# Rotary value projection by Strassen's scheme in a fused perceiver kernel

## The reference, cut to what matters

```python
lat, ctx = layer_norm(latents), layer_norm(context)      # context: 2 x 2048 x 512
q = lat @ Wq                                             # 16 heads of 64
k, v = split(ctx @ Wkv, 2)                               # Wkv: 512 x 2048, so v = ctx @ Wv, Wv 512 x 1024
k = apply_rope(k, cos, sin)
attn = softmax(clip(q @ k.T * 64 ** -0.5, -11, 11))
x = x + (attn @ v) @ Wo + bo
```

## Time and profile before

| | us |
|---|---|
| median of 3 runs (1192.87 to 1197.12) | 1193.29 |
| the profiled execution, its own time | 1196.15 |
| its span, first to last instruction | 1194.4 |

### The profile page before, as it was taken

The page is one execution under the profiler, slowest core; times in us unless marked ns, Lnnn a source line. Parts: engine busy times, 40 slices in busy tenths (PEclk is TensorE's granted clock), DMA queues, the critical chain, the costliest instruction groups (busy, mean ns, idle before and its releaser), DMA issues.

```text
span 1194.4 us, 23415 instructions
## 1 busy us (share of the span) xinstructions
PE 1174.4 (98%) x9888; PEld 963.8 (81%) x9888; DVE 688.8 (58%) x1220; ACT 540.1 (45%) x907; POOL 217.0 (18%) x178
## 2 busy tenths in 40 slices
PE   8999999999999999999899999999999999999998
PEld 6888888888788888864546667888899999999997
DVE  4654554545464533466788885265765566566562
ACT  4433324332433322224359997373644544444441
POOL 2243343444333443350000000010000000000000
PEclk9999999999999999999989999999999999999999
DMA  8210201010100020245232324301545445445440
GB/s 302 71 55 1 66 2 52 4 36 19 36 19 2 27 72 1 83 139 212 96 152 79 136 108 178 142 1 72 228 159 211 161 192 211 157 195 207 158 162 19
DMA packets 28160, 126.06 MB, mean 106 GB/s; under 512 B 2715, under 2 KB 2971, under 8 KB 17572
## 3 DMA queue, kind: packets, MB, share of 16 engines
q1 hardware_dynamic: 28068, 124.74, 27.9%
HBM read 124.20 MB, written 0.52 MB: 104 GB/s over the span
## 4 chain that ended last, share of the span: by engine, by line
PE 49%; issue 2%; DVE 2%; ACT 2%; DVEq 0%
PE mid_bk L57 11%; PE mid_bk L58 10%; PE mid_bk L59 10%; PE mid_bk L1105 5%; PE mid_bk L1120 2%; PE mid_bk L1150 2%; PE mid_bk L1076 2%; PE mid_bk L995 2%; PE mid_bk L1140 1%; PE mid_bk L1249 0%; ACT sa_sc L1415 0%; PE mid_bk L1201 0%; PE mid_bk L1190 0%; PE mid_bk L1050 0%; PE mid_bk L986 0%
## 5 line engine op out<-in xcount | busy, mean ns | idle before, releaser
L565 POOL TENSOR_TENSOR norm_both<-norm_both,prob 128x512 f32<-128x512 f32 x118 | 155.4, 1317 | 145.6 <-DVE prob L357 138.2
L494 ACT ACTIVATE prob<-u_ps 128x512 f32<-128x512 f32 x128 | 66.2, 605 | 181.5 <-PE u_ps L667 181.5
L57 PE MATMUL mid_bk<-mo_x_hi,mo_w_hi 128*128 128x256 f32 x496 | 141.0, 284 | 0.0
L58 PE MATMUL mid_bk<-mo_x_lo,mo_w_hi 128*128 128x256 f32 x496 | 141.0, 284 | 0.0
L59 PE MATMUL mid_bk<-mo_x_hi,mo_w_lo 128*128 128x256 f32 x496 | 141.0, 284 | 0.0
L340 DVE TENSOR_TENSOR turned<-k_ps,tabs 128x512 f32<-128x512 f32 x32 | 22.1, 690 | 189.7 <-PE k_ps L59 189.6
L1788 DVE TENSOR_TENSOR mo_w_lo<-w_raw,mo_w_hi 128x2048 fp32r<-128x2048 f32 x32 | 73.3, 2292 | 72.7 <-ACT mo_w_hi L1497 72.7
L57 PE MATMUL k_ps<-ctx_hi,wk_hi 128*128 128x512 f32 x256 | 102.8, 402 | 0.0
L57 PE MATMUL u_ps<-wv_hi,ctx_hi 128*128 128x512 f32 x256 | 101.7, 397 | 0.8 <-ACT prob L494 0.8
L483 ACT ACTIVATE vals<-u_ps 128x512 f32<-128x512 f32 x64 | 38.3, 598 | 141.2 <-PE u_ps L59 141.1
L1497 ACT ACTIVATE mo_w_hi<-w_raw 128x2048 fp32r<-128x2048 f32 x32 | 61.2, 1913 | 87.9 <-PE mid_bk L59 87.9
(11 more groups left out here) (264 smaller groups left out, 2357.2 us busy)
## 6 DMA issues: line engine op xcount, KB each, us to landing
w_raw<-in_w SPq DMA_DIRECT2D x64, 1024.0 KB, 6.3
ctx_raw<-in_ctx_rows SPq DMA_DIRECT2D x8, 1024.0 KB, 5.5
x_k<-in_ctx_T SPq DMA_DIRECT2D x8, 1024.0 KB, 7.0
x_val<-in_ctx_heads SPq DMA_DIRECT2D x8, 1024.0 KB, 5.0
tabs<-in_rot_tabs SPq DMA_DIRECT2D x8, 512.0 KB, 3.8
vals<-in_wq_rows SPq DMA_DIRECT2D x4, 512.0 KB, 7.6
ctx_raw<-in_wo SPq DMA_DIRECT2D x1, 2048.0 KB, 9.7
x_mask<-in_mask SPq DMA_DIRECT2D x2, 1024.0 KB, 9.0
```

Of the source, the lines that this page charges most:

```text
L57: pe.matmul(out, w_hi, x_hi, start=start, stop=False)
L58: pe.matmul(out, w_hi, x_lo, start=False, stop=False)
L494: act.activation(prob[:, t % 2, i, :], u_ps[:, i, :], ACT.Exp).then_inc(s["exped"], 1)
L565: ins = pool.tensor_tensor(to, to, src, ALU.add)
```

## The change

**The product.** The chunk of context (512 tokens x 512 deep) and Wv (512 x 1024) are cut into 2 x 2 blocks: A11 and A12 are the first 256 tokens, first and second half of the depth, A21 and A22 the other 256; B11, B21, B22 and B12 likewise. Strassen's scheme (Winograd's form) makes the four blocks of v from seven products of blocks in place of eight. V(n, ip), ip = 0 and 1, now does seven products for the ip-th 128 rows of both token halves, at half depth: 2 slices x 3 = 6 matmuls each, 42 in all. Two of the results stay in `u_ps` and a further product is accumulated on them.

**The sums it needs.** The four weight sums T1 to T4 are made once (`weight_sums`). For each chunk DVE makes S1 to S4 in place in `ctx_full` (`sums`, four chained 128x512 operations), ACT rounds them (`high_s`, two of 128x1024), DVE takes the rest (`low_s`, two of 128x1024). The results are joined by `add_products` on DVE (five 128x512 adds from PSUM) and `keep_products` on ACT (two copies), for each ip.

**Memory.** Seven weight blocks take 56 KB a partition, so wk has only two buffers and is loaded and split again at every step (`load_wk`, `high_k`, `low_k`); `ctx_raw` and `tabs` have one buffer each; Wo gets a place of its own and is loaded behind the last V, ahead of the next block's weights; bo, den and the second half of attn_T use other tiles' memory.

**The order.** PE: V(n,0) at the end of step r = 1, behind W; V(n,1) in step r = 2 between K(t) and S(t-1); T(n+1) whole at the head of r = 3.

```diff
-                if t < NT and t % 2 == 0:
...
-                    values(v)
...
+                n, r = t // 4, t % 4
+                if t < NT:
+                    if r == 3 and n + 1 < NC:
+                        for k in range(KD):
+                            transposes(n + 1, k, k)
+                    project(t, 0)
...
+                    project(t, 1)
+                    if r == 2:
+                        values(n, 1)
+                if t >= 1:
                     scores(t - 1)
                 if t >= 2:
                     weigh(t - 2)
+                if t < NT and r == 1:
+                    values(n, 0)
```

In `values(n, ip)` and `scores(t)`:

```diff
+                for bank, (a, w) in enumerate((("A11", "B11"), ("S2", "T2"), ("S3", "T3"), ("S1", "T1"))):
+                    if ip == 0:
+                        pe.wait_ge(s["exped"], 16 * n + bank + 1)
+                    if bank == 1:
+                        pe.wait_ge(s["part_lo"], NWB + 2 * n + 2)
...
+                    product(n, ip, a, w, bank, True, True)
+                pe.wait_ge(s["v_kept"], 2 * v + 1)
+                product(n, ip, "A12", "B21", 0, False, True)
+                pe.wait_ge(s["v_sum"], 5 * v + 2)
+                product(n, ip, "A22", "T4", 2, False, True)
+                pe.wait_ge(s["v_sum"], 5 * v + 3)
+                product(n, ip, "S4", "B22", 3, False, True)
...
+                if t % 4 == 1:
+                    pe.wait_ge(s["v_sum"], 10 * (n + 1))
+                    pe.wait_ge(s["v_kept"], 4 * (n + 1))
```

DVE's loop, and its start ahead of the loop:

```diff
             low_k(0)
+            weight_sums()
+            for j in range(3):
+                low_v(j)
             for t in range(NT + 1):
+                if t < NT and r == 2 and n + 1 < NC:
+                    center(dve, n + 1)
+                if t + 1 < NT:
+                    low_k(t + 1)
                 if t < NT:
+                    if r == 1:
+                        low_s(n)
+                    turn_first(t)
+                    turn_second(t)
+                    if r == 2:
+                        add_products(n, 1)
+                    if t == 0:
+                        for j in range(3, NWB):
+                            low_v(j)
+                    if r == 0:
+                        sums(n)
                 if t >= 1:
                     clip(t - 1)
+                if t < NT:
+                    if r == 1:
+                        add_products(n, 0)
+                    if r == 0 and n + 1 < NC:
+                        stats(dve, n + 1)
+                        spread(dve, n + 1)
```

ACT's (its four query copies stand ahead of `high_k(0)`, as the context's do):

```diff
             queries(2)
             queries(3)
             high_k(0)
+            for j in range(3):
+                high_v(j)
             for t in range(NT + 1):
+                if t < NT and r == 3 and n + 1 < NC:
+                    for k in range(KD):
+                        context(n + 1, k, k)
+                if t + 1 < NT:
+                    high_k(t + 1)
+                if t == 0:
+                    for j in range(3, NWB):
+                        high_v(j)
...
+                if t < NT and r == 2:
+                    keep_products(n, 1)
                 if t >= 1:
                     exponent(t - 1)
+                if t < NT and r == 0:
+                    high_s(n)
+                    if n + 1 < NC:
+                        root(act, n + 1)
+                if t < NT and r == 1:
+                    keep_products(n, 0)
```

POOL does the four `split(n+1)` in step r = 3, ahead of `add_up(t-1)`. SP's loads in the loop:

```diff
+            for t in range(1, NT):
+                n, r = t // 4, t % 4
+                if t + 1 < NT:
+                    load_wk(t + 1)      # waits for K(t-1)
+                if r == 0:
+                    load_tab(n)         # waits for all rotations of chunk n-1
+                if r == 3 and n + 2 < NC:
+                    load_ctx(n + 2)     # waits for T(n+1)
+            sp.wait_ge(s["v_mm"], 2 * NWB * NC)
+            sp.dma_start(wo[:], rows4("wo0")).then_inc(s["wo_in"], 16)
```

More of the change, by code:

```diff
@@ L331, in turn, with weight_sums @@
-            def turn(t):
+            def weight_sums():
+                dve.wait_ge(s["wv_in"], 64)
+                for n, (dst, a, b) in enumerate((("T1", "T3", "B11"), ("T2", "B22", "T1"), ("T3", "B22", "T3"),
+                                                 ("T4", "B21", "T2"))):
+                    dst, a, b = (wv_raw[:, w_of[m], :, :] for m in (dst, a, b))
+                    if n:
+                        dve.wait_ge(s["part_sum"], n)
+                    dve.tensor_tensor(dst, a, b, ALU.subtract).then_inc(s["part_sum"], 1)
@@ new lines, in low_v, with low_k, sums @@
+            def low_v(j):
+                dve.wait_ge(s["part_hi"], j + 1)
+                dve.tensor_tensor(wv_lo[:, j, :, :], wv_raw[:, j, :, :], wv_hi[:, j, :, :],
+                                  ALU.subtract).then_inc(s["part_lo"], 1)
+            def low_k(t):
+                dve.wait_ge(s["wk_hi"], t + 1)
+                dve.tensor_tensor(wk_lo[:, t % 2, :, :], wk_raw[:, t % 2, :, :], wk_hi[:, t % 2, :, :],
+                                  ALU.subtract).then_inc(s["wk_lo"], 1)
+            def sums(n):
+                dve.wait_ge(s["csplit"], 4 * n + 4)
+                for m, (dst, a, b, op) in enumerate((("A22", "A21", "A22", ALU.add), ("A21", "A11", "A21", ALU.subtract),
+                                                     ("A11", "A22", "A11", ALU.subtract),
+                                                     ("A12", "A12", "A11", ALU.subtract))):
+                    if m:
+                        dve.wait_ge(s["part_sum"], 4 + 4 * n + m)
+                    dve.tensor_tensor(full[dst], full[a], full[b], op).then_inc(s["part_sum"], 1)
@@ L574, in _ @@
                 n = t // 4
-                if t < NT and t % 2 == 0 and n + 1 < NC:
-                    for kk in range(2):
-                        split(n + 1, 2 * (t % 4 // 2) + kk)
+                if t < NT and t % 4 == 3 and n + 1 < NC:
+                    for k in range(KD):
+                        split(n + 1, k)
                 if t >= 1:
@@ L633, in project, with product @@
[L633 to L646 removed]
+            def product(n, ip, a, w, bank, start, stop):
+                src, kh, th = a_of[a]
+                rows = slice(256 * th + ip * P, 256 * th + ip * P + P)
+                for kk in range(2):
+                    k = 2 * kh + kk
+                    hi, lo = ((ctx_hi[:, n % 2, k, rows], ctx_lo[:, n % 2, k, rows]),
+                              (s_hi[:, k, rows], s_lo[:, k, rows]))[src]
+                    for part_a, part_b in ((hi, wv_hi), (hi, wv_lo), (lo, wv_hi)):
+                        ins = pe.matmul(u_ps[:, bank, :], part_a, part_b[:, w_of[w], kk, :],
+                                        start=(start and kk == 0 and part_a is hi and part_b is wv_hi),
+                                        stop=(stop and kk == 1 and part_a is lo), skip_group_check=True)
+                ins.then_inc(s["v_mm"], 1)
```

361 lines of the change are left out of this document (166 added, 195 removed).

## The result

The change makes the kernel slower: 1222.89 us median (1221.69 to 1225.54, 4 runs) beside 1193.08 for the kernel before on the same chip (1191.97 to 1197.12, 4 runs), a ratio of 1.0247 with a 95% interval of 1.0216 to 1.0277. That is +29.8 us where +14.5 was forecast: the right direction, twice the size, and above the range of 1197 to 1219. The profiled execution ran 1221.69 us.

A forecast was written before the change was run, and what follows sets the result against it. PE's own matmuls were taken as the bound, busy 98% of the span. Terms -21.8 + 8.8 + 8.4 + 0.7 + 17.4 + 1.0 gave +14.5 us on the 1193.3 median: 1207.8 us, range 1197 to 1219.

The forecast's parts named there:

- Saving: PE's value products: 84 matmuls a chunk instead of 96, at 0.227 us each over 8 chunks, -21.8 us.
- rival 3: Value matmuls: the saving isn't there because the new ones lose their pitch, up to +21.8 us, 1230; chance 0.04.
- Wait ahead of the scores: S(4n+1) behind V(n,1) waits for the last `add_products`: 1.1 us for each of 8 chunks, +8.8 us.
- The start: Before V(0,0), PE waits for ACT's and DVE's preparation in three gaps: +17.4 us, bounds 14 and 20.
- The clock's +1.0: Slow PE matmuls after idling at the start: +1.0 us, bounds 0 to 3.
- Wait inside V(n,0): Product 6 waits for DVE's second add: 1.4 us in each of six chunks, +8.4 us.
- Splits: POOL's four context splits come slightly late for K(4n+4): +0.7 us for seven chunks, bounds 0 and 7.
- The forecast's base: Whole kernel: the profiled execution before ran 1196.15 us, 2.9 over the median, so the forecast started from the 1193.3 median.
- context for the next chunk: Preparing the next chunk ends in time except POOL's splits, needed by K(4n+4): +0.7 us, bounds 0 and 7.
- rival 1: DVE's chain is longer, +0.3 us per two-input SBUF operation beside busy POOL, splits late as well: 1219; chance 0.17.
- a table switch at 2.66 us: ACT's table load before V(n,0): the skill's figure would add some 1.5 us overall; the prediction used the trace's 1.28.

The follow-up runs named there:

- e3: Changed kernel with POOL's denominator additions taking one column of 128 per block, nearly all those sums left out: 1201.78 us, ratio 1.0079.
- e1: Changed kernel with ACT taking the next chunk's root behind the exponentials instead of ahead of them: 1223.98 us, ratio 1.0248.
- e2: Changed kernel with POOL making the four splits ahead of the previous step's `add_up` instead of behind it: 1236.11 us, ratio 1.0350.
- e5: Changed kernel with two of the four splits moved from POOL to DVE, at the head of step r = 3: 1223.64 us, ratio 1.0268.
- i1: h3 with two calls exchanged, `sums` of the next chunk ahead of `clip` instead of behind it: 1191.09 us, ratio 0.9975.
- h3: Changed kernel with V(n,1) between K(4n+2)'s halves, later moments, reordered start, earlier `sums`, `low_s` ahead of `clip`, all splits on POOL: 1199.78 us, ratio 1.0056.
- f1: Changed kernel with V(n,0) and V(n,1) back to back between K(4n+2)'s halves, root, product adds and `center` moved: 1240.32 us, ratio 1.0413.

## Why the prediction was right, and where it failed

**Saving: right.** The value matmuls kept their pitch (128.96 to 130.09 is five, 0.226 each). 96 fewer are the 21.8 us; rival 3 is out.

**Wait ahead of the scores: right.** 7.9 us in 8 waits, each with its restart about 1.1; predicted 8.8.

**The start: right.** Gaps of 2.89, 5.01 and 5.63 us where 3, 5 and 8 were named, K(0) at 30.15 (30.5), K(1) at 40.90 (41.3), V(0,0) at 56.70 (57.2). V(0,0) ends near 67.8 for 67.9. Slow matmuls were expected behind all three gaps and came behind the last two: the first twelve of K(1) at 40.90 and the first seven of V(0,0) at 56.70 stood 0.43 apart, those behind the gap of 2.89 us at 0.23. S(0) so ended 2.2 later than charged (51.0 for 48.8), which is why the third gap was 5.6 and not 8. The clock's +1.0 is inside the 67.8, so charging it on top was too much.

**Wait inside V(n,0): the place right, the term too small.** Charged 1.4 a chunk; in this one product 6 starts 2.6 later than without waits, in two pieces. K(4n) at 0, here 162.82; the measured column is from the timelines of DVE, ACT and PE:

| | predicted | measured |
|---|---|---|
| second key half visible | 5.8 | 5.8 |
| `sums` begin | 8.2 | 9.2 |
| `clip(4n-1)` begins | 11.0 | 12.0 |
| root begins | 15.8 | 17.6 |
| first exponential begins | 18.3 | 20.0 |
| V(n,0) starts | 19.2 | 20.7 |
| product 6 starts | 27.0 | 28.6 |

The chain is the predicted one, operation by operation, but for the size of two: L398, 1.06 longer, and L306, 1.10 longer, both beside POOL. Together 2.2; the steps between were 0.4 shorter than charged, V(n,0) had 0.3 to spare, and it starts 1.5 late. Chunk 7 was charged nothing, as it has no moments; there `low_k` and `low_s` ran beside POOL (2.13 and 4.53), and V(7,0) waited 1.0 for `s_lo` and 0.5 at product 6.

**Splits: the term was mis-sized, and for the same reason.** Charged 0.1 a chunk: 7 x 0.1. The four splits start at 156.22; at the 5.3 of e3 they would end at 161.5, and K(4n+4), ready at 161.46, would be 0.1 late, as forecast. They took 6.50 and K was 1.36 late. Five of seven chunks show this.

The terms for the changed block: -21.8 saved; start +17.3 with its clock (67.8 - 49.7 - 0.8); S(4n+1) 8 x 1.14, 9.1; V(n,0) and product 6 in chunks 1 to 7, some 16; K(4n+4), some 8. (The last two are the idle times of 13.8 and 7.2 with some 0.1 to 0.2 for each restart, an estimate.) That makes some +28.6, and the trace has +28.4. Against the forecast of +14.5 the last two are 15 more (24 for 9.1) and the start 1.1 less. The forecast's base was right too: before's profiled execution had a slow stretch of its own and I set it off.

**The step that failed** is the price of two engines side by side, in the terms "wait inside V(n,0)" (+8.4, some 16 measured) and "context for the next chunk" (+0.7, some 8 measured). I read "beside POOL a subtract of 512 columns 0.98 for 0.68" as the most it could cost, and made rival 1 from +0.3 for each operation. That step had met only the end of POOL's work: it starts at 321.67, and POOL's splits there end at 322.10. The trace of before showed the full price at a place that I had left out because nothing waited there: `center`, four operations beside `add_up`:

```profile
84.81 5.14 DVE L310 TENSOR_SCALAR ctx_raw<-ctx_raw,cmv,crs 128x512 f32<-128x512 f32 x4
...
85.44 4.22 POOL L565 TENSOR_TENSOR norm_both<-norm_both,prob 128x512 f32<-128x512 f32 x3
```

Alone such four take 1.92 (at 195.33 in after, with POOL idle). Rival 1, a longer DVE chain at 1219, had the right mechanism and half the price, and its counter-argument, that POOL is idle for most of the chain, looked at POOL's share and not at what releases it: every `add_up` starts with the clip that DVE has just made, so it runs beside whatever DVE does next.

Two smaller points. I summed the waits at V(n,0) and at K(4n+4) as independent; e1, e2 and e5 show them to be tied, as two ends of one chain. And the page that puts a table switch at 2.66 us (the Trainium skill, ScalarE: Activation LUTs, What ACT_TABLE_LOAD costs) was rightly left out of the sum; ACT's timeline of after has 1.28 and the exponential behind it at once:

```profile
180.38 0.20 ACT L318 ACTIVATE csd<-cva 128x4 f32<-128x4 f32 x1 [2.13 <-DVE cva L306]
180.49 1.04 ACT L513 ACTIVATE wk_hi<-wk_raw 128x1024 fp32r<-128x1024 f32 x1
181.55 1.28 ACT L557 ACT_TABLE_LOAD   x1
182.84 1.58 ACT L557 ACTIVATE prob<-u_ps 128x512 f32<-128x512 f32 x3
```

## What to carry to other kernels

Fewer matmuls are worth their pitch only if the work that replaces them stays off the chain that releases PE; here 21.8 us saved on PE cost 50 in waits as written, and came out as a gain of some 6 (0.5%) only with the moments, sums, splits, V(n,1) and the start moved. When DVE and POOL both read SBUF, look at which DVE operation releases POOL, and put behind it what reads PSUM and ahead of it what must be done quickly. A wait that disappears in one place and returns at another in every single mend points to one chain: lengths have to be taken off it, not moved along it.

## What the hardware showed that I had not expected

- DVE and POOL side by side: 0.68 to 1.75 for a two-input step of 512 columns, 0.17 to 1.27 for a step of four columns, 2.86 to 5.76 for four chained, while POOL's four went from 5.4 to 6.8 or 7.1. Steps that read PSUM kept 0.68 beside a busy POOL.
- The step of four columns has one SBUF input, as have `clip` (2.52 for 1.42 at 171.85 in i1) and `center`, so a second input isn't needed for the loss.
- One exchange of two calls with no change of work was worth 8.7 us of 1200 (h3 to i1).
- After 4.15 us of idleness in a busy stretch (f1) the granted clock was 0.50 for 3.1 us; after gaps of 2.13 us and less (V(n,0) in after) the first matmul took 0.50 for 0.39, and from 120 us to the end of the block the clock was 1.00.
